# A cross-attention and mixture-of-experts layer on one core: keys projected in place of queries and values, attention in slots of one token tile, all gate/up weights resident, experts in two halves of the tokens

## The reference

```python
# block 1: attention over the context, 8 heads, then a small ffn
q = einsum('bsd,hdk->bhsk', layernorm(x), Wq);  k = einsum('btd,hdk->bhtk', ctx, Wk)
v = einsum('btd,hdv->bhtv', ctx, Wv)
A = softmax(m * (q k^T) + (1 - m) * -1e30)
proj = concat_heads(A v) @ Wo
x1 = layernorm(ctx + proj) * gamma0 + beta0
x  = x + layernorm(x1 + relu(x1 @ W1 + b1) @ W2 + b2) * gamma1 + beta1
# block 2: 16 routed experts (top 4 in the top 2 of 4 groups) and 2 shared ones, F = 128
xm = layernorm(x)
combine = route(sigmoid(xm @ router_w.T))            # [tokens, 16]
y = sum_e combine[:, e] * ((silu(xm @ gate_e) * (xm @ up_e)) @ down_e)
x = x + y + shared(xm)
```

## Time and profile before

| | us |
|---|---|
| median of 3 runs | 342.14 (341.71 to 342.58) |
| the profiled execution | 341.1 |
| its span, first to last instruction | 339.4 |
| PE busy | 314.8 (93%) |
| DVE busy | 220.9 (65%) |
| ACT busy | 145.5 (43%) |
| POOL busy | 92.0 (27%) |
| moved by DMA | 26.79 MB |

### The profile page before, as it was taken

One profiled execution on the slowest core, in us unless ns is written; L12 is line 12 of the kernel. 1 busy time (PEld: TensorE's weight loads), 2 busy tenths in 40 slices (PEclk: granted clock), 3 DMA queues, 4 the chain that ended last, 5 costly groups with the idle time before them and its releaser, 6 DMA issues.

```text
span 339.4 us, 5140 instructions
## 1 busy us (share of the span) xinstructions
PE 314.8 (93%) x1611; PEld 240.6 (71%) x1611; DVE 220.9 (65%) x568; ACT 145.5 (43%) x266; POOL 92.0 (27%) x105
## 2 busy tenths in 40 slices
PE   3989899999999998986977999999999999999993
PEld 3979789788978896874655666666666666666662
DVE  2818526948895789798676835566566656565654
ACT  2664673477347734662325342333333233333320
POOL 3006413634473444453263042000000000000000
PEclk9999999999999999999997999999999999999999
DMA  8996000000000000002100046333233333323004
GB/s 243 349 272 214 3 0 3 0 0 2 1 3 0 2 0 2 0 4 74 57 0 1 2 138 240 124 116 106 95 118 124 124 124 124 122 114 102 32 0 124
DMA packets 18773, 26.79 MB, mean 79 GB/s; under 512 B 1330, under 2 KB 13124, under 8 KB 18628
## 3 DMA queue, kind: packets, MB, share of 16 engines
q1 hardware_dynamic: 16676, 25.52, 22.8%
q10 hardware_dynamic: 2080, 1.05, 1.1%
HBM read 25.38 MB, written 1.18 MB: 78 GB/s over the span
## 4 chain that ended last, share of the span: by engine, by line
PE 76%; DVE 12%; ACT 4%; issue 3%; POOL 2%; DMA 1%; DVEq 0%; POOLq 0%; ACTq 0%
PE bank L1331 17%; PE bank L1059 12%; PE bank L1061 12%; PE bank L1060 12%; PE bank L1144 8%; PE bank L1122 7%; DVE cen L725 3%; PE bank L1171 2%; DVE sc_m L768 2%; ACT prob_T L525 2%; PE bank L1201 1%; DMA wqk_in<-in_L_xattn_Wq 1%; ACT v_o L510 1%; DVE stat L709 1%; ACT hid L535 1%
## 5 line engine op out<-in xcount | busy, mean ns | idle before, releaser
L646 ACT ACTIVATE wT<-bank 128x512 f32<-128x512 f32 x72 | 43.0, 597 | 84.9 <-PE bank L1061 84.8
L1059 PE MATMUL bank<-mT_hi,we_hi 128*128 128x512 f32 x128 | 74.0, 578 | 3.9 <-DVE wT L992 2.0
L992 DVE TENSOR_TENSOR wT<-bank,wT 128x512 f32<-128x512 f32 x64 | 44.1, 691 | 39.5 <-PE bank L1061 29.8
L1061 PE MATMUL bank<-mT_hi,we_lo 128*128 128x512 f32 x128 | 50.5, 394 | 0.0
L1060 PE MATMUL bank<-mT_lo,we_hi 128*128 128x512 f32 x128 | 50.3, 393 | 0.0
L1059 PEld LDWEIGHTS bank<-mT_hi,we_hi 128*128 128x128 f32 x128 | 24.0, 188 | 22.0 <-issue 12.3
L398 POOL TENSOR_TENSOR we_lo<-w_exp,we_hi 128x256 fp32r<-128x256 f32 x16 | 11.8, 740 | 97.8 <-ACT we_hi L567 97.8
L1331 PE MATMUL bank<-wT,we_dn 128*128 128x512 f32 x72 | 37.5, 605 | 0.0
L1331 PE MATMUL bank<-q_T,we_dn 128*128 128x512 f32 x72 | 36.5, 592 | 0.0
L1060 PEld LDWEIGHTS bank<-mT_lo,we_hi 128*128 128x128 f32 x128 | 24.1, 188 | 16.7 <-issue 14.0
L1122 PEld LDWEIGHTS bank<-cT_m,q_T 128*128 128x128 f32 x256 | 30.3, 192 | 6.4 <-DVE sc_m L768 5.9
(11 more groups left out here) (181 smaller groups left out, 529.9 us busy)
## 6 DMA issues: line engine op xcount, KB each, us to landing
wvo_in<-comb_dram SPq DMA_DIRECT2D x16, 512.0 KB, 3.5
wqk_in<-comb_dram SPq DMA_DIRECT2D x15, 512.0 KB, 3.6
mask_row<-in_mask_BxS_ff SPq DMA_DIRECT2D x1, 1024.0 KB, 8.8
out_x<-ctx_all SPq DMA_DIRECT2D x4, 256.0 KB, 2.8
x_all<-in_x SPq DMA_DIRECT2D x1, 768.0 KB, 8.2
ctx_all<-in_ctx SPq DMA_DIRECT2D x1, 768.0 KB, 10.5
wqk_in<-in_L_xattn_Wq ACTq DMA_DIRECT2D x1, 512.0 KB, 4.8
wqk_in<-in_L_xattn_Wk ACTq DMA_DIRECT2D x1, 512.0 KB, 5.6
```

The costliest lines, as they stand in the source:

```text
L646: a.activation(silu[k % 2], h_bank[k % 2][:], ACT.Silu).then_inc(silu_ready, 1)
L992: v.tensor_tensor(s_u[k % 2], u_bank[k % 2][:], silu[k % 2], ALU.mult).then_inc(s_u_ready, 1)
L1059: pe.matmul(dst, w_hi, m_hi, start=start, stop=False)
L1061: return pe.matmul(dst, w_lo, m_hi, start=False, stop=stop)
```

## The change

Parts of the algorithm and of the order change together.

- Weights and inputs come laid out by the host: Wq, Wk and Wv are already turned, in pairs and halves (`w_in`), so the 24 transposes go. x, the context and the output have each partition's rows next to each other. The mask comes as a column for each token and as rows for 64 partitions.
- The folded Wq Wk^T is applied to the masked context instead of to x: `key(c, h)`, 8 heads, `three` each, 96 matmuls of 512 columns as the queries had. Keys of chunk c+1 are made during the slots of chunk c.
- `values` go (96 matmuls of 512 columns). `attend` multiplies the probabilities with the context itself, four f32 matmuls of 256 columns for a tile, which have 64 rows each (row tiles: partitions 0 to 63 and 64 to 127, alternating; `ctx_swap` is a second copy of the context with the halves of a tile exchanged, one more MB loaded). Two ACT copies (`heads_out`) bring the result to SBUF, and `project` multiplies by the folded Wv Wo: 8 f32 matmuls of 128x128 for a tile, added up in one bank.
- `scores`: two f32 matmuls of 512 columns for a tile, each with 64 stationary columns (column tiles: output partitions 0 to 63 and 64 to 127 of one bank), instead of eight of 128 columns.
- `spread` is one copy of 128x512. `normalise` for 1 and 3 moves from DVE to ACT, with a `shift` computed on POOL and a `neg_mean` on DVE.
- A single loop over 16 slots (one tile each) orders all engines. The odd keys share the bank of the scores.
- All 18 experts' gate/up weights are split ahead, two experts at a time, in nine of the slots, from a stage that is loaded three times; down weights are used as loaded. No split, no copy of weights in the expert steps.
- 72 expert steps, all unrolled: chunks 0 and 1 for all experts, then chunks 2 and 3. All weighing is on POOL. The last chunk's ffn, normalisation and routing lie in steps 0 to 24. Routing weights come in a ring of four of 1024 tokens. The outputs of chunks 0 and 1 are turned, added and stored in the middle of the second half.

The diff, cut to its core:

```diff
-            for i, ready in enumerate((ld_wq, ld_wk, ld_wv)):
-                pe.wait_ge(ready, 16)
-                for half in range(2):
-                    for h in range(HP):
-                        src = wqk_in[:, i, half * HP + h, :] if i < 2 else wv_in[:, half * HP + h, :]
-                        last = pe.transpose(bank[2 * i + half][:, h * P:(h + 1) * P], src, ident[:])
-                    last.then_inc(w_turned, 1)
...
+        we_hi, we_lo = sb("we_hi", [P, NX, GU], F32R), sb("we_lo", [P, NX, GU], F32R)
...
+        comb = [k_flat[0][:, i * HALF:(i + 1) * HALF] for i in range(RING)]
+        act = [k_flat[1][:, i * CW:(i + 1) * CW] for i in range(4)]
+        silu = [xnT[:, i * CW:(i + 1) * CW] for i in range(2)]
+        s_u = [xnT[:, i * CW:(i + 1) * CW] for i in range(2, 4)]
+        acc_out = [o_flat[c // 2][:, c % 2 * CW:(c % 2 + 1) * CW] for c in range(CH)]
...
+        acc = [bank[3], bank[6], bank[2], bank[7]]
+        key_bank = [bank[0], sc_bank]
+        h_bank, u_bank = bank[0:2], bank[4:6]
...
+        def order(a, b):
+            first = [(e, c) for c in (a, b) for e in range(NSH)]
+            last = [(e, c) for c in (a, b) for e in (NX - 2, NX - 1)]
+            return first + [(e, c) for e in range(NSH, NX - 2) for c in (a, b)] + last
...
+        SPLITS = [3, 4, 5, 7, 8, 9, 11, 12, 13]
...
+            context(0, 1, ld_c0)
...
+            rows(0, 1, ld_x0)
+            context(1, 2, ld_c1)
+            for r in range(2):
+                sp.dma_start(mask_add[r * half_p:(r + 1) * half_p].rearrange("p t s -> p (t s)"),
+                             mask_pairs[r].partition_broadcast(half_p)).then_inc(ld_mask, 16)
+            for half in range(2):
+                sp.dma_start(w_in[:, 1, half], w_attn[:, 1, half]).then_inc(ld_w[1][half], 16)
+            swapped(0, 1, ld_swap0)
+            rows(1, 2, ld_x1)
...
+            rows(2, CH, ld_x)
+            swapped(1, CH, ld_swap)
+            sp.dma_start(vec_row[:], vec.partition_broadcast(P)).then_inc(ld_vec, 16)
...
+            sp.wait_ge(fold_done, 4)
+            for i in range(NX // BATCH_E):
+                if i:
+                    sp.wait_ge(gu_lo_ready, i * BATCH_E // 2)
+                sp.dma_start(stage, w_gu[:, i * BATCH_E:(i + 1) * BATCH_E, :]).then_inc(ld_gu, 16)
+                if i == 0:
+                    sp.dma_start(dn, w_dn).then_inc(ld_dn, 16)
...
+            for m in range(NT):
+                c, p = divmod(m, TPC)
+                subtract_max(m)
+                if c == 0 and p + 1 < CH:
+                    inverse_root(0, p + 1)
+                if p == 2 and c >= 1:
+                    inverse_root(1, c - 1)
...
+                    mask_context(c + 2)
+                if p == 3 and c >= 1:
                     add_b2(c - 1)
+                if m in SPLITS:
+                    split_lo(SPLITS.index(m))
...
+            inverse_root(2, CH - 2)
             inverse_root(3, CH - 2)
+            inverse_root(1, CH - 1)
+            add_beta(CH - 1)
+            for n in range(N):
+                if n == 5:
+                    add_b2(CH - 1)
+                if weighted(n):
...
+            def heads_out(n):
+                if n >= 2:
+                    a.wait_ge(av_full, n - 1)
                 for j in range(2):
+                    a.wait_ge(o_full[j], n + 1)
+                    a.copy(o_T[n % 2][:, j].rearrange("p h s -> p (h s)"), o_bank[j][:]).then_inc(o_taken[j], 1)
...
+            for m in range(NT):
+                c, p = divmod(m, TPC)
+                ahead = c + 1 < CH
+                if ahead:
...
+                    a.wait_ge(ld_vec, 16)
+                    a.wait_ge(ld_small, 16)
+                if p == 2 and c >= 2:
+                    normalise(3, c - 2, tokens(x2, c - 2))
+                if p == 3 and c >= 1:
+                    normalise(1, c - 1, tokens(y, c - 1))
+                    turn_x1(c - 1)
+                exponent(m)
+                if ahead:
+                    key(c + 1, 2 * p + 1)
...
                     xm_high(c - 2)
+                if p == 3 and c + 2 < CH:
+                    cT_high(c + 2)
+                if p == 3 and c >= 1:
                     hidden(c - 1, 0)
+                if m >= 1:
+                    spread(m - 1)
...
+            router_sigmoid(0)
+            spread(NT - 1)
+            heads_out(NT - 1)
...
+            for m in range(NT):
+                c, p = divmod(m, TPC)
+                if m >= 3:
+                    add_ctx(m - 3)
+                mask_and_max(m)
+                if c == 0 and p + 1 < CH:
+                    if p < 2:
...
                     residual(c - 2)
+                if p == 2 and c >= 1:
                     v.wait_ge(y_ready, c * TPC)
                     statistics(1, c - 1, tokens(y, c - 1))
...
+            add_ctx(NT - 3)
+            bias_scores(0)
+            add_ffn(CH - 2)
+            statistics(2, CH - 2, z)
+            group_scores(0)
+            keep_groups(0)
+            add_ctx(NT - 2)
+            residual(CH - 2)
+            keep_experts(0)
             statistics(3, CH - 2, tokens(x2, CH - 2))
+            combine(0)
+            for n in range(N):
+                gate_up(n)
+                if n == 0:
+                    add_ctx(NT - 1)
+                    v.wait_ge(y_ready, NT)
+                    statistics(1, CH - 1, tokens(y, CH - 1))
+                if n == 1:
+                    take_combine(0)
+                if n == 4:
+                    mT_low(CH - 2)
...
+            def key(c, h):
+                i = h % 2
+                if c == 0 and h % HP == 0:
+                    pe.wait_ge(fold_lo, h // HP + 1)
+                if h == 0:
+                    pe.wait_ge(key_free[0], ctx_use(c))
+                elif key_use(c, h) > 1:
+                    pe.wait_ge(key_free[i], key_use(c, h) - 1)
+                if i == 1 and c:
+                    pe.wait_ge(sc_taken, (c - 1) * TPC + h // 2 + 1)
+                three(key_bank[i][:], qk_hi[:, h, :], qk_lo[:, h, :], cT_hi[:], cT_lo[:], True, True
+                      ).then_inc(key_full[i], 1)
...
+            def scores(n):
+                c, p = divmod(n, TPC)
                 if p == 0:
+                    pe.wait_ge(key_free[0], key_use(c, NH - 2))
+                    pe.wait_ge(xn_taken, c + 1)
+                odd = key_use(c, NH - 1) + (p if c + 1 < CH else 0)
+                pe.wait_ge(key_free[1], odd)
+                if n:
+                    pe.wait_ge(sc_taken, n)
                 for s in range(2):
                     b = 2 * p + s
+                    tok = n * P + s * SEQ
+                    pe.matmul(sc_bank[s * SEQ:(s + 1) * SEQ, :], xnT[:, tok:tok + SEQ],
...
+            def attend(n):
+                pe.wait_ge(prob_T_ready, n + 1)
+                if n:
+                    for j in range(2):
+                        pe.wait_ge(o_taken[j], n)
+                for s in range(2):
+                    for j in range(2):
+                        rows = slice(j * SEQ, (j + 1) * SEQ)
+                        held = ctx_all if s == j else ctx_swap
+                        last = pe.matmul(o_bank[j][:].rearrange("p (h b s) -> p h b s", b=2, s=SEQ)[:, :, s, :],
+                                         held[rows, n, :], prob_T[n % 2][rows, :, s, :], start=True, stop=True)
+                        if s == 1:
+                            last.then_inc(o_full[j], 1)
...
+            def project(n):
                 for j in range(2):
+                    pe.wait_ge(o_taken[j], n + 1)
+                if n:
+                    pe.wait_ge(y_ready, n)
                 for h in range(NH):
+                    last = pe.matmul(av_bank[:, 0:P], o_T[n % 2][:, h % 2, h // 2, :], vo[:, h, :],
...
+            for m in range(NT):
+                c, p = divmod(m, TPC)
+                ahead = c + 1 < CH
+                scores(m)
+                if ahead:
+                    key(c + 1, 2 * p)
+                if m == 0:
+                    fold(1, 0)
+                if c == 0 and p >= 1:
+                    turn_xn(p)
+                if p == 0 and c >= 2:
+                    ffn_down(c - 2)
+                if p == 3 and c >= 1:
...
+                    if c == 1:
+                        pe.wait_ge(ld_ffn, 32)
+                    ffn_up(c - 1, 0)
+                if m >= 1:
+                    turn_probs(m - 1)
+                if m == 2:
+                    pe.wait_ge(fold_hi, 4)
+                if m >= 2:
+                    project(m - 2)
...
+                    pe.wait_ge(ld_swap0, 32)
+                if m == TPC + 1:
...
+            ffn_down(CH - 2)
+            turn_probs(NT - 1)
+            project(NT - 2)
+            attend(NT - 1)
+            pe.wait_ge(sc_taken, NT)
+            up(0)
+            pe.wait_ge(logits_ready, 2)
+            up(1)
+            project(NT - 1)
+            for n in range(2, N):
+                if n == 2:
+                    turn_combine(0)
```

(35 more changed lines are left out.)

1231 lines of the change are left out of this document (470 added, 761 removed).

## The result

The changed kernel takes 342.82 us (median of 12 runs, 341.41 to 344.63) where the kernel before took 341.82 beside it (12 runs, 341.12 to 342.58): ratio 1.0031 [1.0016, 1.0047], slower by 0.3%, at the edge of what the forecast wanted to count as no change. The forecast was 337.0, 1.4% faster, so its sign was wrong; that 342.8 lies inside its range of 324 to 354.5 says little, since the range also held 342.1. The profiled execution took 342.44 with a span of 340.7; it was forecast as 335.1.

A forecast was written before the change was run, and what follows sets the result against it. PE, busy 93%, was taken to bound the kernel before. Start 15.4, slots with drains 123.5, passage 18, clock 1.7, experts 166.9 + 4 and end 5.6 gave 335.1 span, 337 us in all; likeliest 329 to 342, full range 324 to 354.5.

The forecast's parts named there:

- The change takes no work off PE: All PE work: removed and added products balance at about 0 us if matmuls on different array halves don't overlap.
- s + a = 2.36: Each tile's scores (1.29) plus attend (1.07), in us, with partial overlap by record order; bounds 1.72 and 3.44.
- Changes of mode, 0.16 each: Switching the array between whole and tiled products before each tile's scores: 16 x 0.16 = 2.6 us, the upper end.
- A slot is s + 4.57 + a.: Plain loop slot: scores, 4.57 us until ACT's spread releases attend, then attend; 6.93 us in all.
- Moved work on ACT is costed at nothing but where named: Loop slots: work moved to ACT mostly adds no time; POOL carries at most about 8 us in slot 9.
- The hand-overs in a slot are longer than the clean chain: Rival: 0.5 us more per slot, or a longer DVE row before the experts; 8 us, total 345; chance 0.11.
- perfect pairs: Rival on scores and attend: tiles overlap fully, 1.72 us together, 10.2 us off, total 327; chance 0.22.
- Tiles don't overlap, 354: Rival on scores and attend: no overlap, 3.44 us together, 17.3 us more, total 354, slower; chance 0.22.
- The start, 15.4: Kernel start: first scores at 15.4 us, was 22.5; first fold at 5.2, keys from 8.55.
- The passage, 18 with 7 of wait: Between slots and experts: combine ends 18 us after the last slot; PE waits some 7 us at turn_combine(0).
- the clock, 1.7: After the wait between slots and experts: PE's granted clock falls once, losing 1.7 us.
- Experts and end: Expert steps at 2.25 us, 166.9 in all, plus 4 for DVE's routing pieces; then 5.6 to the end.

The follow-up runs named there:

- experiment 3: Changed kernel with attend's loops over s and j exchanged, so products on the same rows follow one another: 341.46 us, ratio 1.0013.
- Experiment 7: Changed kernel with spread and odd key before exponent, weight splits on DVE, reordered passage: 334.84 us; second kernel also reorders slots with p = 2 and 3: 324.42.
- experiment 1: Changed kernel with project over four of eight heads: 341.49 us, ratio 0.9994; with project run twice: 357.62 us, ratio 1.0433.
- experiment 5: Changed kernel with the nine low splits of gate/up weights moved from POOL to DVE, behind each slot's maximum: 343.12 us, ratio 1.0019.
- experiment 2: Changed kernel with all score products on one half of the array's columns and all attend products on one half of its rows: 361.68 us, ratio 1.0595.
- Experiment 6: Changed kernel with the first four expert products ahead of DVE's residual and statistics, ACT's and POOL's due steps moved by three: 338.38 us, ratio 0.9888.

## Why the prediction was wrong, step by step

The sum for the span in its terms, and what the trace of the changed kernel has for each (us):

| | forecast | measured |
|---|---|---|
| first scores | 15.4 | 18.0 |
| slots 0 to 3 | 25.8 | 27.2 |
| slots 4 to 7 | 31.2 | 32.5 |
| slots 8 to 11 | 33.7 | 37.9 |
| slots 12 to 15 | 30.2 | 33.1 |
| the 16 changes of mode | 2.6 | in the slots |
| passage | 18 | 15.8 |
| clock, experts | 172.6 | 171.5 |
| end | 5.6 | 4.7 |
| span | 335.1 | 340.7 |

**"The change takes no work off PE" unless halves overlap, s + a = 2.36.** The bounds were right (1.72 and 3.44), the choice between them was not: 2.08 was measured, near the pairs' end, and 3.76 alone. Its reason, that order decides which neighbours overlap, fell with experiment 3. By itself this miss would have made the kernel 4.5 us faster than forecast (16 x 0.28). (The range of 324 to 354.5 isn't this term's either: 16 x 0.64 off 336.8 is 326.6.)

**Changes of mode, 0.16 each.** From the last pair of `attend` to the scores the starts are 52.05 - 51.74 = 0.31 apart where two records of `attend` are 0.22 apart: 0.1 us. The first product behind the scores starts 0.33 before the second (53.06, 53.39) instead of 0.23. So about 0.1 at each, and the measured 2.08 already contains it, so the 2.6 us of the forecast were counted for nothing. The Trainium skill, TensorEngine Tiling (Array Packing), section Key Properties, states that a change of tiling mode drains the array; the trace shows no more than this 0.1 beside it.

**"A slot is s + 4.57 + a."** This is the step that failed, not in the plain slots (6.98 against 6.93, though with 2.08 in it the sum gives 6.65, so the hand-overs cost 0.33 more) but in the claim that it carries over: **"Moved work on ACT is costed at nothing but where named, and POOL carries at most about 8 us in the densest slot (9), which is where its cover ends."** The cover was measured by the amount of work in a slot. What counted was its place in an in-order queue. In slot 10 POOL had 2.9 us of work that nobody waited for ahead of the subtraction, in the slots with p = 2 and 3 PE stood at `turn_xm` and `turn_x1` (9.0 us in all, 0.6 of it behind the loop) with ready products behind, and ACT held `spread` behind the exponent (most of the 9.0 us of waiting at `attend`).

The loop took 7.2 us more than forecast although tiles were 4.5 cheaper and the 2.6 for changes of mode weren't needed: some 14 us that the sum had not. They don't lie evenly. Slots 8, 9 and 12 came within 0.15 us of their forecast; against the forecast with 2.08 put in, slots 1, 10, 11, 13 and 14 alone are 10.8 us longer. Experiment 7 took most of the 14 us back without touching the arithmetic (in its second kernel the first product behind the loop, `ffn_down`, starts at 136.98 instead of 149.70), which shows that the order of the queues was the cause, with the clock that follows from it; experiment 1 shows that it was not PE's work.

**The clock in the loop.** The second step that failed: the forecast took the lower clock once, for the passage, and none in the loop. In fact PE fell to it four times there. PE after, columns: stretch, length, PE busy, granted clock, DMA share, GB/s:

```profile
28.00:34.00 6.00, 4.79 (x20) 0.72 0.20 81
105.00:112.00 7.00, 4.78 (x19) 0.76 0.00 0
128.00:134.50 6.50, 4.45 (x19) 0.74 0.00 0
134.50:138.20 3.70, 3.70 (x22) 0.54 0.00 0
...
164.50:168.60 4.10, 4.10 (x11) 0.50 0.05 13
```

The four in the loop lie behind waits of 2.10, 2.22, 2.60 and 2.02 us, in slots 1, 11, 13 and 14. So a hand-over in the slots costs its own length and then a slower PE besides. In slot 14 the 16 records of `project` took 3.45 us (134.68 to 138.13) instead of 1.80. An estimate of what the falls cost together: the loop has some 14 us at the lower clock, worth at most half, 7 us. The changed kernel's runs with a mean clock of 0.979 and of 0.963 differ by about 2.5 us in time and by 11 us at the lower clock (0.016 x 2 x 340), which would make it 3. The rest of the 14 us is waiting. A wait of this length was not always followed by a fall; the changed kernel first, then the kernel of experiment 5, both behind a wait of 2.22 us at `turn_x1` in slot 7:

```profile
70.00:74.00 4.00, 3.27 (x21) 1.00 0.02 4
```
```profile
70.00:74.00 4.00, 3.92 (x13) 0.57 0.00 0
```

**The rivals.** "The hand-overs in a slot are longer than the clean chain" (0.5 us for each slot, 8 us, chance 0.11) comes nearest: 14 us, 0.9 a slot on average, but with most of it in five slots and part of it the clock. It met tiles cheaper than forecast, near the rival "perfect pairs", and a shorter passage, so that the errors partly cancelled. That the total came within 6 us of the forecast is luck; no single case of it held, and that two could be true together was not among the cases. "Tiles don't overlap, 354" is excluded: in the changed kernel s + a is 2.08, and the kernel in which they don't overlap (experiment 2) took 361.7.

**The start, 15.4.** Measured 18.0. PE's first fold waited for its load until 5.64 (forecast 5.2), keys began at 10.03 (8.55), because DVE's split of the context ended there, and x was turned at 15.17, released by DVE's normalisation. The load was right to 0.5; the chain from the fold to the keys took 4.4 us where 3.35 were counted, and then pauses between the keys and the late turning of x cost the rest, 1.1 us (7.96 from the first key to the scores, 6.85 counted).

**The passage, 18 with 7 of wait, and the clock, 1.7.** The gap was 4.68, the passage 15.8; the clock fell as forecast. Experiment 6 shows it worth 4.4 us together.

**Experts and end.** 2.25 us a step as forecast; the allowance of 4 us for DVE's routing pieces wasn't needed in full (1.1 less). The end was 0.9 shorter.

## What to carry to other kernels

When PE work is removed from a stage that other engines nearly fill, draw up what each queue holds ahead of the operation that PE waits for: position in the queue, not the amount of work, decides whether it is hidden, and leaving out still more PE work shows whether PE was the bound (here 14.4 us gave 1.3). Put what is ready first (copies of finished banks ahead of an exponent that waits; products whose operands lie ready ahead of a transpose that waits), and take the wait at the far end of the slot. Look at the granted clock behind each wait as well as at the wait: here it was part of the price, and it moved with every experiment. Keep rivals apart that work on different terms: two of them can both be true and cancel.

## What the runs showed of the hardware

- Two f32 matmuls on different halves of the array take hardly longer than one: the two of the scores 1.01 us in a pair against 1.86 on one half (0.93 each), the four of `attend` 1.07 against 1.90, whatever the order in which the products of a half are queued (experiment 3).
- The same normalisation on DVE (four of 128x128) took 1.11 us while POOL was idle, and 2.82 while POOL worked:

```profile
124.62 2.82 DVE L706 TENSOR_SCALAR cen<-x_b,mean_var,rstd_g 128x128 f32<-128x128 f32 x4
...
157.39 1.11 DVE L706 TENSOR_SCALAR cen<-x_b,mean_var,rstd_g 128x128 f32<-128x128 f32 x4
```

  POOL's own operations lengthen too (1.35 instead of 1.05 beside DVE's split in experiment 5), so work moved from one of the two to the other can come back as time.
- Waits of PE of 2.02 to 2.60 us in a busy loop were followed by the lower granted clock (1.2 GHz) four times in one execution; a wait of 2.22 us was followed by a fall in one kernel and by none in another (slot 7, above), and one of 1.87 us (before 101.18) by none. The length of the last wait alone didn't decide.
